# Two-layer cross-attention network with routed experts: z and x3 stored and gathered as one row, row-number copies ahead of the transfers

## What is computed

```python
x = x + _L0_xattn_ref(_layernorm(x), ctx, ctx, mask)     # attention, 16 heads of 16
x = x + _L0_ffn_ref(_layernorm(x), w_gate, w_up, w_down)  # quantised feed-forward
x = x + _L1_xattn_ref(_layernorm(x), ctx, ctx, Wq, ...)   # attention, 16 heads of 64
x = x + _L1_ffn_ref(_layernorm(x), W1, b1, W2, b2, Wr, br)

def _L1_ffn_ref(x, W1, b1, W2, b2, Wr, br):
    indices = jnp.argmax(softmax(x @ Wr + br), axis=-1)
    out = 0
    for i in range(8):
        xi = x * (indices == i)[..., None]
        out = out + (relu(xi @ W1[i] + b1[i]) @ W2[i] + b2[i])
    return out
```

## Time and profile before

| | |
|---|---|
| median of 3 runs | 1664.19 us (1663.76 to 1664.63) |
| the profiled execution, its own time | 1662.31 us |
| its span | 1660.6 us |
| PE busy | 1414.4 us, 85% |
| DVE busy | 1276.8 us, 77% |
| ACT busy | 1008.6 us, 61% |
| POOL busy | 438.7 us, 26% |
| mean granted TensorE clock | 0.941 of full speed |

### The profile page before, as it was taken

How to read it: one execution, slowest core, us unless ns; L and a number is a source line. 1 busy time by engine, 2 the same in 40 slices (tenths; PEclk the granted TensorE clock), 3 DMA queues, 4 the chain that set the end, 5 groups by cost and what they waited for, 6 DMA issues and landing times. The chain is left out here.

```text
span 1660.6 us, 35783 instructions
## 1 busy us (share of the span) xinstructions
PE 1414.4 (85%) x11323; PEld 1195.4 (72%) x11323; DVE 1276.8 (77%) x2223; ACT 1008.6 (61%) x2527; POOL 438.7 (26%) x638
## 2 busy tenths in 40 slices
PE   3899999879985019789999999999999649989897
PEld 2455555558863019789998888989898539988897
DVE  6988888766869897657777777777777579978786
ACT  2466656545559636366667666766666318867675
POOL 3211111100000000212232222222222256667666
PEclk9999999979999559899999999999999769999999
DMA  5311011000024103510111111111101057111110
GB/s 194 121 57 31 28 32 28 27 1 0 1 66 136 38 0 112 156 76 24 33 33 50 35 32 32 36 40 32 32 29 33 27 222 299 44 44 43 45 47 16
DMA packets 66241, 96.75 MB, mean 58 GB/s; under 512 B 10214, under 2 KB 57327, under 8 KB 63346
## 3 DMA queue, kind: packets, MB, share of 16 engines
q1 hardware_dynamic: 60546, 83.16, 15.3%
q0 software_dynamic: 5616, 12.60, 2.4%
HBM read 76.57 MB, written 21.90 MB: 59 GB/s over the span
## 5 line engine op out<-in xcount | busy, mean ns | idle before, releaser
L1668 ACT ACTIVATE c_w_raw<-c_ps_score,c_shift 128x128 f32<-128x128 f32 x512 | 184.7, 398 | 133.1 <-DVE c_shift L1520 125.1
L2061 PE MATMUL d_ps_hT<-d_zT,d_w_tile 128*128 128x128 f32 x1248 | 148.3, 278 | 2.1 <-DVE d_zT L2166 2.1
L2061 PEld LDWEIGHTS d_ps_hT<-d_zT,d_w_tile 128*128 128x128 f32 x1248 | 145.2, 195 | 2.7 <-DVE d_zT L2166 2.7
L805 PE MATMUL b_ps<-b_down_high,b_inner 128*128 128x256 f32 x384 | 71.0, 289 | 87.8 <-DVE b_inner L1087 87.8
L362 PE MATMUL a_ps_score<-a_keys,a_qT 128*128 128x512 f32 x256 | 137.1, 618 | 3.9 <-ACT a_qT L552 2.2
L2232 ACT ACTIVATE d_h<-d_ps_hT,d_b1T 128x128 f32<-128x128 f32 x312 | 88.7, 367 | 64.8 <-PE d_ps_hT L2061 63.8
L2074 PE MATMUL d_ps_y<-d_w_parts,d_hT 128*128 128x256 f32 x936 | 124.4, 290 | 1.8 <-DVE d_res L2193 1.8
L805 PEld LDWEIGHTS b_ps<-b_down_high,b_inner 128*128 128x128 f32 x384 | 60.7, 194 | 88.1 <-issue 88.1
L1668 ACT ACTIVATION_READ_ACCUMULATOR c_w_raw<-c_ps_score,c_shift 128x1 f32 x512 | 121.1, 237 | 0.0
L2185 DVE TENSOR_TENSOR d_w_parts<-d_w,d_w_parts 128x1024 fp32r<-128x1024 f32 x78 | 95.8, 1229 | 31.4 <-ACT d_w_parts L2244 27.2
L2074 PEld LDWEIGHTS d_ps_y<-d_w_parts,d_hT 128*128 128x128 f32 x936 | 117.2, 195 | 2.4 <-DVE d_res L2193 2.0
(11 more groups left out here) (260 smaller groups left out, 3743.1 us busy)
## 6 DMA issues: line engine op xcount, KB each, us to landing
d_w<-w_in SPq DMA_DIRECT2D x16, 1024.0 KB, 10.2
b_x_space<-w_in SPq DMA_DIRECT2D x16, 512.0 KB, 3.6
a_x<-x_in SPq DMA_DIRECT2D x4, 1024.0 KB, 7.6
a_keys<-ctx_blocks_in SPq DMA_DIRECT2D x128, 32.0 KB, 2.1
a_v_raw<-ctx_in SPq DMA_DIRECT2D x4, 1024.0 KB, 8.3
x_scratch<-a_x SPq DMA_DIRECT2D x32, 128.0 KB, 1.7
b_x_space<-x_scratch SPq DMA_DIRECT2D x32, 128.0 KB, 2.5
x_scratch<-b_x_space SPq DMA_DIRECT2D x32, 128.0 KB, 1.9
```

Source lines behind the costliest of these rows:

```text
L805: last = pe.matmul(ps[:, t, 0:D], inner[:, s, a, f, t * P:(t + 1) * P], down_parts[b][:, f, :], start=(j == 0), stop=(j == NF * len(PARTS) ...
L1668: last = act.activation(prob[:, n, j, :], ps_score[:, n % 2, j, :], ACT.Exp, scale=float(KD) ** -0.5, bias=shift[:, n, j:j + 1], accum_out ...
L2061: last = pe.matmul(ps_hT[:, f, :], w1_tile[:, half, k, n * P:(n + 1) * P], zT[:, s, k, :], start=(k == 0), stop=(k == ND - 1))
```

## The change

attention1 writes x3 and z side by side into one buffer zx of four slots, each slot 512 numbers wide, z in the first half and x3 in the second. SP stores both with one DMA per tile, 256 KB instead of two of 128 KB, at the place where z was stored. A slot has one semaphore, zx_stored, and x3 waits for it; z has no wait of its own.

experts gathers z and x3 with one indirect DMA per tile, whose rows are 2 KB long. Since the slot holds x3 too, the gather for tile j+2 now waits for two things: z_turned of tile j-1, and residual_taken of tile j-1.

DVE's finish is cut in two. `residual` for tile j stands before the second L2185 of step j and puts x3 + other[expert] into res. `finish` for tile j-1 adds the PSUM result to it with one instruction. Its sign to PE that the PSUM result has been read (y_read) is now res_ready.

In a step of POOL both row-number copies come first, then the gather, then the scatter.

```diff
--- before.py
+++ after.py
@@ attention1, SP, per tile
-                    if inside(b, 3, NB + 2):
-                        sp.wait_ge(x3_ready, b - 2)
-                        sp.dma_start(x3_dram[b - 3], x3[:, (u + 1) % 4, :]).then_inc(x3_stored[(u + 1) % 4], 16)
                     if inside(b, 4, NB + 3):
                         sp.wait_ge(z_ready, b - 3)
-                        sp.dma_start(z_dram[b - 4], z[:, u, :]).then_inc(z_stored[u], 16)
+                        sp.dma_start(zx_dram[b - 4], zx[:, u, :]).then_inc(zx_stored[u], 16)
@@ attention1, DVE
-                        dve.wait_ge(x3_stored[u], 16 * (uses(t, i) - 1))
+                        dve.wait_ge(zx_stored[u], 16 * (uses(t, i) - 1))
...
-                        dve.wait_ge(z_stored[u], 16 * (uses(t, i) - 1))
@@ experts, POOL
+                def copy_zx_ids(j, s, i):
+                    uses = held(16 * i)
+                    if inside(j, NS, NT - 1):
+                        pool.wait_ge(zx_gathered[s], uses)
+                    pool.tensor_copy(zx_ids[:, s:s + 1], ids[:, bass.ds(j, 1)]).then_inc(zx_ids_ready, 1)
+
+                def copy_out_ids(j, s, i):
+                    uses = held(16 * i)
+                    if inside(j, NS, NT - 1):
+                        pool.wait_ge(out_stored[s], uses)
+                    pool.tensor_copy(out_ids[:, s:s + 1], ids[:, bass.ds(j, 1)]).then_inc(out_ids_ready, 1)
+
+                def gather(j, s):
+                    ready, back = held(j + 1), held(j - NS + 1)
                     pool.wait_ge(ids_ready, 1)
                     if inside(j, NS, NT - 1):
                         pool.wait_ge(z_turned, back)
-                        pool.wait_ge(z_gathered[s], uses)
...
+                        pool.wait_ge(residual_taken, back)
+                    pool.wait_ge(zx_ids_ready, ready)
+                    index = bass.IndirectOffsetOnAxis(zx_ids[:, s:s + 1].bitcast(U32), 0)
+                    pool.indirect_dma_start(zx[:, s, :], None, zx_dram, index, bounds_check=last_token, oob_is_err=False)\
+                        .then_inc(zx_gathered[s], 16)
...
                 def step(j, s, i):
                     if inside(j, 0, NT - NS):
-                        gather_z(j + 2, (s + 2) % NS, i if s == 0 else i + 1)
-                    if inside(j, 0, NT - 1):
-                        gather_x3(j, s, i)
+                        copy_zx_ids(j + 2, (s + 2) % NS, i if s == 0 else i + 1)
                     if inside(j, 2, NT + 1):
-                        scatter(j - 2, (s + 1) % NS, i if s == 2 else i - 1)
+                        copy_out_ids(j - 2, (s + 1) % NS, i if s == 2 else i - 1)
+                    if inside(j, 0, NT - NS):
+                        gather(j + 2, (s + 2) % NS)
+                    if inside(j, 2, NT + 1):
+                        scatter(j - 2, (s + 1) % NS)
 
-                gather_z(0, 0, 0)
-                gather_z(1, 1, 0)
+                pool.wait_ge(ids_ready, 1)
+                for j in range(2):
+                    copy_zx_ids(j, j, 0)
+                for j in range(2):
+                    gather(j, j)
@@ experts, PE
-                        pe.wait_ge(y_read, j)
+                        pe.wait_ge(res_ready, j)
@@ experts, DVE
-                def finish(j, s, i):
-                    e = expert_of(dve, j)
-                    dve.wait_ge(w2_used, 2 * (j + 1))
+                def residual(j, s, i, e):
                     if inside(j, NS, NT - 1):
                         dve.wait_ge(out_stored[s], 16 * i)
-                    dve.tensor_tensor(res[:, s, :], ps_y[:, 0:D], other[:, e, :], ALU.add).then_inc(y_read, 1)
-                    dve.wait_ge(y_read, j + 1)
-                    dve.wait_ge(x3_gathered[s], 16 * (i + 1))
-                    dve.tensor_tensor(res[:, s, :], res[:, s, :], x3[:, s, :], ALU.add).then_inc(res_ready, 1)
+                    dve.wait_ge(zx_gathered[s], 16 * (i + 1))
+                    dve.tensor_tensor(res[:, s, :], zx[:, s, D:2 * D], other[:, e, :], ALU.add).then_inc(residual_taken, 1)
+
+                def finish(j, s):
+                    dve.wait_ge(w2_used, 2 * (j + 1))
+                    dve.wait_ge(residual_taken, j + 1)
+                    dve.tensor_tensor(res[:, s, :], ps_y[:, 0:D], res[:, s, :], ALU.add).then_inc(res_ready, 1)
...
                     if inside(j, 1, NT):
-                        finish(j - 1, (s + NS - 1) % NS, i if s else i - 1)
+                        finish(j - 1, (s + NS - 1) % NS)
                     if inside(j, 0, NT - 1):
+                        residual(j, s, i, e)
                         low_w2(j, 1, e)
```

More of the change, by code:

```diff
@@ L1102, with attention1 @@
 INNER_C = NH * KD
[L1105 removed]
+def attention1(nc, ident, mv2, rstd2, logits, wq_raw, wq_address, w, ctx_t, x2_dram, zx_dram, finished):
     BLKS = INNER_C // P
@@ L1190, in attention1 @@
         late_loaded = [sem(f"late_loaded{s}") for s in range(4)]
-        x3_stored = [sem(f"x3_stored{s}") for s in range(4)]
-        z_stored = [sem(f"z_stored{s}") for s in range(4)]
+        zx_stored = [sem(f"zx_stored{s}") for s in range(4)]
         consts = sem("consts")
@@ L1768, with experts @@
 assert NT % NS == 0
-def experts(nc, ident, logits, idle_dram, w, z_dram, x3_dram, out):
+def experts(nc, ident, logits, idle_dram, w, zx_dram, out):
     FB = FE // P
@@ L1877, in experts @@
         tile_expert_ready = sem("tile_expert_ready")
-        z_gathered = [sem(f"z_gathered{s}") for s in range(NS)]
-        x3_gathered = [sem(f"x3_gathered{s}") for s in range(NS)]
+        zx_gathered = [sem(f"zx_gathered{s}") for s in range(NS)]
         z_turned = sem("z_turned")
-        z_ids_ready = sem("z_ids_ready")
-        x3_ids_ready = sem("x3_ids_ready")
+        zx_ids_ready = sem("zx_ids_ready")
         out_ids_ready = sem("out_ids_ready")
@@ L1965, in held @@
                     return value if isinstance(value, int) else pool.to_reg(value)
-                def gather_z(j, s, i):
-                    ready, back, uses = held(j + 1), held(j - NS + 1), held(16 * i)
+                def copy_zx_ids(j, s, i):
[10 more added lines that the diff above has]
+                    ready, back = held(j + 1), held(j - NS + 1)
                     pool.wait_ge(ids_ready, 1)
@@ L2261, in cross_attention_network @@
 def cross_attention_network(nc, eye, x, ctx, ctx_blocks, ctx_t, mask_t, w_up, w_gate, w_down, w, experts_w, out):
-    x1, x2, x3, z = (nc.dram_tensor(f"{name}_scratch", [NB, P, D], F32).ap() for name in ("x1", "x2", "x3", "z"))
+    x1, x2 = (nc.dram_tensor(f"{name}_scratch", [NB, P, D], F32).ap() for name in ("x1", "x2"))
+    zx = nc.dram_tensor("zx_scratch", [NB, P, 2 * D], F32).ap()
     idle = nc.dram_tensor("idle_scratch", [NE, D], F32).ap()
@@ L2296, in cross_attention_network @@
                                  experts_w["w2"], idle, address, wq_raw, w["wq"], used)
-        attention1(nc, ident, mv2, rstd2, logits, wq_raw, wq_address, w, ctx_t, x2, x3, z, used)
-        experts(nc, ident, logits, idle, experts_w, z.rearrange("b p d -> (b p) d"), x3.rearrange("b p d -> (b p) d"), out)
+        attention1(nc, ident, mv2, rstd2, logits, wq_raw, wq_address, w, ctx_t, x2, zx, used)
+        experts(nc, ident, logits, idle, experts_w, zx.rearrange("b p n -> (b p) n"), out)
 def kernel(**inputs):
```

53 lines of the change are left out of this document (13 added, 40 removed).

## The result

The changed kernel took 1637.95 us (median of 4 runs, 1637.67 to 1639.86), the kernel before 1663.97 us beside it. The ratio is 0.9847, with a 95% interval of 0.983 to 0.9864. The forecast was 1637.7 us.

What follows compares the result with a forecast made beforehand. POOL's queue, 7.85 us per tile against PE's 6.67, was taken as the bound. -27.9 - 1.6 + 2.5 + 0.5 = -26.5 us takes 1662.3 to 1635.8, or 1637.7 us as median; range 1633 to 1649 us.

Steps and rivals of the forecast that it cites:

- 25 slow periods: Expert loop, tile 13 to 38: each period of 7.78 us becomes PE's 6.67 us, 27.9 us saved.
- start: copies ahead, longer landing: Start of experts: first gather ends 1.9 us later, held by DVE's L2217, plus 0.6 us for the larger transfer: 2.5 us cost.
- the store at the end of attention1: End of attention1: the last store, now 256 KB, holds the stage's end and takes 0 to 1.2 us longer; 0.5 taken.
- last scatter, last second layer: End of experts: with one addition and POOL caught up, the last scatter starts at 1655.1 instead of 1656.74 us; 1.6 us saved.
- POOL's cycle of 7.85 us: Expert loop: per tile 3.98 us of transfers, 1.42 of copies, 2.45 of idle time; the change makes it 5.0 us.
- The copies first ... nothing.: POOL's loop: copies wait for transfers of three tiles ago and run in 1.67 us of free time; no effect except at the start.
- The price of 2-KB rows: Merged gather: POOL's time taken as unchanged (1.418 us; 2.84 if paid per byte), landing 0.6 us longer.
- The slot freed later: Loop: z's gather also waits for residual of the tile three before; the way takes 5.35 of 8.1 us; no cost.
- The 2.7 us to spare: Loop: what remains of 8.1 us from slot release to need after a way of 5.35 us.
- The rival with the late gathers: Loop until about 1410 us: under weight loads the period is 7.15 us for 6 tiles, 2.9 us more, 1641 us; chance 0.05.
- the prediction's own list: Signs of a wrong prediction: PE waits for zx in loop, DVE's gaps vanish while PE waits, or gather exceeds 2.9 us.
- The 1.9 us added for the median: Whole kernel: the median lies 1.9 us above the profiled execution, so 1635.8 us becomes 1637.7 us.

## Why the prediction was right, and where it wasn't

The total was right to 0.3 us. The parts were less so:

| step | predicted | measured in the profiled execution |
|---|---|---|
| 25 slow periods | -27.9 | -28.1 |
| late gather while weights load | 0 (a rival: +2.9) | +1.2 |
| start: copies ahead, longer landing | +2.5 | +0.6 |
| the store at the end of attention1 | +0.5 | 0.0 |
| last scatter, last second layer | -1.6 | -3.2 |
| DRAIN | not seen | +5.2 |
| sum | -26.5 | -24.3 |

The end of the changed kernel, its last second layer, last addition and last scatter:

```profile
1622.78 3.23 PE L2059 MATMUL d_ps_y<-d_w_parts,d_hT 128*128 128x256 f32 x24 [1.78 <-DVE d_res L2182]
...
1626.05 0.42 DVE L2182 TENSOR_TENSOR d_res<-d_ps_y,d_res 128x256 f32<-128x256 f32 x1 [1.85 <-PE d_ps_y L2059]
1627.28 0.98 POOL L1985 DMA_INDIRECT out<-d_res,d_out_ids  x1 [2.04 <-DVE d_res L2182]
```

- **The bound and the floor.** POOL's cycle of 7.85 us, with its idle time counted, was the period, and PE's 6.67 us was the floor. Both stand, and the sum of the gain with them. The steps that failed moved single microseconds.
- **"The copies first ... nothing."** True within this change, false as a reading of the profile. The 0.8 us of idle time ahead of each transfer was taken for a fixed price of a transfer. Yet the earlier trace rows names its cause in two of three lines, "POOL d_z_ids" and "POOL d_x_ids", the copy just ahead. Had the idle time been split, 0.3 us for a transfer and 0.5 for the copy, the cycle with the copies first would have come out at 7.85 - 1.5 = 6.35 us, under PE's 6.67, and the second way to the same gain would have been on paper. The 0.3 us could not be read before: in the old kernel every transfer has its copy right ahead, and the size of the split was first seen in the trace of the changed kernel. But a rival with it was missing.
- **The price of 2-KB rows.** Unchanged on POOL, as taken (1.19 us). For the landing, 0.6 us were taken; at the start it is 2.35 instead of 1.83 us, so 0.52. The experiments repeat both: 2.3 to 2.4 us in the kernels with the merge, 1.8 to 1.9 in the others. By the Trainium skill (DMA: Bandwidth & Descriptors, Anatomy of one DMA — SWDGE (gpsimd) path) it would be 0.3 us; the measurement lies nearer to the slices of the earlier trace rows.
- **The slot freed later.** The first piece of the way was measured as taken: residual ends at 1375.43 us and its gather starts at 1376.29, 0.86 against 0.87 us. The 2.7 us to spare hold in the loop, but 7.36 us of landing while weights load uses them up once. The rival with the late gathers was right in its mechanism, with one tile instead of six. By the prediction's own list a wait of PE for zx in the loop would have shown it wrong; there was this one, of 1.02 us.
- **The start.** The mechanism was right, as one copy more shows, but the position was not. The second copy costs nothing, as it runs while the first transfer waits for its own copy. The step that failed is "the copy for tile 1 stands before it, at least 0.2 us". A row for it was there: the 0.97 us of idle time in the earlier trace rows. With one copy more the gather does end 2.2 us later against the start of the sorting, near the 1.9 us of the prediction.
- **The store.** SP was through with waiting for its stores 0.3 us later than before, at 1325.8 instead of 1325.5 us. But DVE's last instruction of attention1 starts only at 1326.0 in both kernels, and it ends the stage. The step that failed is "Only the last store holds the end of the stage".
- **The end.** The earlier scatter came, 0.81 us behind VectorE's last addition, as against 0.87 predicted. The other 1.4 us are the last second layer, 3.23 instead of 4.62 us at granted clock 1.00 instead of 0.50. The early residual does not decide it, since with it the clock was 1.00 in four kernels of the table and 0.50 in two. Without it, it was 0.50 in all four; whether the edit makes the full clock likelier stays open.
- **The DRAIN.** It was missing altogether: the end of the block behind the last scatter was put at nothing, and it costs 5.2 us. That the total was still right is luck: the errors of the start, the end and the store, 4.0 us, nearly pay for the DRAIN and the late gather, 6.4 us. Set against its own execution the forecast is 2.3 us too low (1635.8 against 1638.07 us). The 1.9 us added for the median closed the rest, and the profiled execution of the changed kernel was not below its median.

## What to carry to other kernels

Split an engine's idle time by what ended it before calling it a price: a wait for the instruction right ahead can be had back by a change of order alone, here 0.5 us for each of three copies. In this kernel that alone brought the 28 us that merging two tensors brought. When two repairs of one bound both reach the next bound, only the first of them is worth anything, so try the cheaper one alone. And look at what stands behind the last useful instruction: here the kernel with 78 transfers had a longer end than the one with 117.

## What the runs showed of the hardware

- An indirect DMA on POOL starts 0.8 us behind the copy that writes its row numbers, if that is right ahead, and 0.30 us behind another transfer. Behind the VectorE instruction that it waits for it starts 0.81 to 0.87 us later.
- POOL's time for a gather of 128 rows does not grow with the row: 1.0 us at 1 KB and at 2 KB where it is shortest. The means in the loop are 1.19 us at 2 KB and 1.07 to 2.01 at 1 KB.
- The DRAIN of POOL at the end of this block was 6.44 us with 78 indirect transfers, 7.10 with 86 and 8.57 with 104, 0.082 us for each. At the 114th transfer POOL stops for 2.0 to 3.7 us, and the DRAIN is 1.1 to 1.2 us at 117 and 4.5 us at 156.
- A gather that starts 0.04 us behind a long two-input instruction of VectorE takes 1.36 us, and one that starts 0.15 us behind it 3.48 us.
